# Statistics of x first, x1's normed rows made late on VectorE, values' products ahead of the maxima, in a fused GNN and attention kernel

## The chip, the cores and the metric

One NeuronCore of a Trainium2 chip runs the program. The metric is the device time in microseconds of one execution. TensorE is PE here (PEld its weight loads), VectorE is DVE, ScalarE is ACT, GpSimd is POOL, and SP issues all the DMAs.

## The reference

x has 1250 rows (nodes) of 512. What is computed, cut to what matters:

```
xn = layernorm(x)
x1 = x + relu(xn @ W_self.T + mean_of_neighbours(xn) @ W_neigh.T + b)      # 41250 edges
       + linear_attention(xn) @ W_out.T + b_out                            # softmax of k over rows
z  = layernorm(x1)                                   # input of the last block
route = softmax(gelu(mean_rows(z) @ r1.T + b) @ r2.T + b)   # picks one spatial, one temporal expert
s = spatial_expert(ln(z)); t = temporal_expert(ln(z))       # 8 heads of 64, temporal one causal
z = z + cross_attention(s, t)
out = x1 + z + mlp(ln(z))                            # 512 -> 2048 -> 512
```

## The kernel before

Rows lie in ten tiles of 125 (`NT`), features in four blocks of 128. Precise products are made of three: every operand is split into a rounded part (hi) and the rest (lo), and hi*hi, hi*lo and lo*hi are added in PSUM. POOL splits the weights: it casts `w_raw` to `w_hi` (L893) and subtracts (L895); SP loads them three slots ahead. Semaphores order everything; each engine's program is a fixed list.

**Start.** SP issues the edges, x in three transfers (blocks of 4, 4 and 2 tiles, `TB`), `vecs`, six one-row transfers into `raw_rows`, then the weights. VectorE makes the edge keys, waits for the six rows (L1527), makes `row_mix`, `row_gnn` and `ones_r` of them (L1528 to L1534), and only then the statistics of x (`bn_stats`, L1538), the aggregates, with a square root on ScalarE in between (L1084), and ten normed tiles (L1448, `normed`). `to_feature` on PE (L1926) turns them into features through two PSUM banks (6 and 7), ScalarE copies the hi part (L1092), VectorE subtracts for the lo part (L1458). Then the first key products run (L1975).

**Edges.** Forty windows: VectorE makes one-hot rows (L1558, L1559), PE counts with them (L2076), and side products of the linear attention and the GNN are placed between. x1 is in `kept`; VectorE takes its statistics. The last tile's neighbour sum (`neighbours`, L2042) has `set_turn` (L1941) placed between its parts: these turn `set_rows`, x1 normed twice, into features, copied by `set_in` on ScalarE and `set_lo_in` on VectorE.

**Router.** POOL makes x1's normed rows z into `tok_b` (L982, nine tiles; VectorE makes the tenth). PE takes their mean with a column of 1/1250 (L2107), VectorE copies it out (L1638), two small products, a gelu and a softmax follow; SP reads the two expert numbers into registers and loads the experts' biases and weights. `tok_b` is also stored to DRAM (`d_xn`, 2000 KB at L776 and 500 KB at L811), since z is added again near the end. x1 itself is stored to `d_x1`.

**Passes.** Twelve passes of two heads each (0 to 3 spatial, 4 to 7 temporal, 8 to 11 cross) with up to 50 steps (S scores, P products with the values), planned by due times. Each pass needs keys (K, three pieces), queries (Q, five tiles), values (V, three pieces), maxima (M, ten for a query tile), their row turned (R, L2227) and the values turned (T). Inside a run of passes these are spread over the steps of the pass before. Passes 0 and 8 have no pass before them, so an order written out by hand opens them (`OPENING`); PE's waits there are for ScalarE's copies of the keys (L1221) and VectorE's reductions of the maxima (L1718, L1727). A head pair's output of a query tile is scaled by `unit_out` on VectorE (L1735, L1737).

**End.** When all queries are made, SP loads `tok_z` from `d_xn` and `bias_out`; POOL adds the bias to each tile (L1034). The last output goes through `oc_hi` (ScalarE), `oc_lo` (VectorE, L1818), the projection (L2328), the sum with `tok_z` (L1828), a layer norm and the MLP.

Of the kernel before, what the change touches and what calls it, by code (L numbers as in the profile page):

```python
# [6 lines left out]
F32 = mybir.dt.float32  # L7
# [11 lines left out]
TOK = 125  # L19
# [138 lines left out]
def value_turns(n):  # L158
# [4 lines left out]
OPENING = {n: [("K", n, 0), ("K", n, 1), ("K", n, 2), ("Q", n, 0)] + maxima(n, 0)[0:2] + [("V", n, 0)] + maxima(n, 0)[2:4] + [("V", n, 1)]  # L163
           + maxima(n, 0)[4:6] + [("V", n, 2)] + maxima(n, 0)[6:8] + [("Q", n, 1)] + maxima(n, 0)[8:] + [("R", n, 0)] + value_turns(n)
# [151 lines left out]
def load_order():  # L316
# [12 lines left out]
    events += [(AT["F", x], 0, ("fold", x)) for x in range(FB)] + [(AT["Q", 3, 4], 0, ("xt",)), (28, 0, ("store",)), (-1, NO["v", 0] + 0.5, ("rows",))]  # L329
# [59 lines left out]
def build(nc, A, out):  # L389

    ctx = ExitStack()
    with ctx:
# [111 lines left out]
        tok_b = sb("tok_b", [TOK, NT, D], F32, tok_b_at)  # L504
        set_rows = sb("set_rows", [TOK, NT, D], F32)
# [5 lines left out]
        mean_col = sb("mean_col", [TOK, 1], F32)  # L511
# [113 lines left out]
        s_tok = sem("s_tok")  # L625
# [111 lines left out]
        def _(sp):  # L737
# [5 lines left out]
            sp.dma_start(vecs[:, :], A["vecs"]).then_inc(s_ld_vec, 16)  # L743
# [14 lines left out]
            for k in range(16):  # L758
                weights(k, block_of("w_gps", k))
# [15 lines left out]
            sp.wait_ge(s_tok, 8)  # L775
            sp.dma_start(d_xn[:, 0:8, :], tok_b[:, 0:8, :]).then_inc(s_st_xn, 16)  # L776
# [21 lines left out]
            for what, *at in LOADS:  # L798
# [9 lines left out]
                if what == "rows":  # L808
                    sp.wait_ge(s_tok, FIRST_ROWS)
                    sp.wait_ge(s_ln_done, 2 * NT - 1)  # L810
                    sp.dma_start(d_xn[:, 8:NT, :], tok_b[:, 8:NT, :]).then_inc(s_st_xn, 16)  # L811
# [15 lines left out]
            sp.wait_ge(s_st_xn, 32)  # L827
            sp.dma_start(tok_z[:, :, :], d_xn).then_inc(s_xn_back, 16)
# [36 lines left out]
        def _(pool):  # L865
# [79 lines left out]
            pool.memset(mean_col[:, :], 1.0 / NODES).then_inc(s_const, 1)  # L945
# [52 lines left out]
            pool.wait_ge(s_st_xn, 32)  # L998
# [77 lines left out]
        def _(act):  # L1076
# [9 lines left out]
            def features_in():  # L1086

                m = 0
                for t0, nt in TB:
                    for f in range(FB):  # L1090
                        act.wait_ge(s_tr, m + 1)
                        act.activation(xa_hi[:, f, t0 * TOK:(t0 + nt) * TOK], ps[:, 6 + m % 2, 0:nt * TOK], ACT.Copy).then_inc(s_tr_act, 1)  # L1092
                        m += 1

            def set_in(m):
# [6 lines left out]
                if f == FB - 1:  # L1102
                    act.wait_ge(s_st_first, 16)
                    act.wait_ge(s_tok, 2)
                act.activation(z_feat[:, f, span], src, ACT.Copy).then_inc(s_tr_act, 1)

            ln_root(0)
# [213 lines left out]
            act.wait_ge(s_st_xn, 32)  # L1321
# [84 lines left out]
        def _(dve):  # L1406
# [44 lines left out]
            def features_lo():  # L1451

                m = 0
                for t0, nt in TB:
                    for f in range(FB):
                        span = slice(t0 * TOK, (t0 + nt) * TOK)
                        dve.wait_ge(s_tr_act, m + 1)
                        dve.tensor_tensor(xa_lo[:, f, span], ps[:, 6 + m % 2, 0:nt * TOK], f32(xa_hi[:, f, span]), ALU.subtract)\  # L1458
# [1016 lines left out]
```

## Time and profile before

| what | value |
|---|---|
| runs | 1999.69, 1993.12, 1999.56 us; median 1999.56 |
| profiled execution | 1993.96 us; span 1992.2 us |
| mean granted TensorE clock | 0.977 |
| PE busy | 1824.9 us, 92% |
| DVE, ACT, POOL busy | 1181.7, 723.5, 356.4 us |
| DMA | 60.56 MB, 30 GB/s on the mean |

The span runs from the first to the last instruction of the profiled execution. Times in the rows are counted from its start. In a timeline row the first two numbers are start and duration; "x8" means that eight instructions in a row are merged; the bracket tells how long the engine was idle before and what ended that. In the chain, each piece is what the end of the program hung on at that time.

### The profile page before, as it was taken

To read this page: it belongs to the slowest core of one execution; us is meant where nothing else is said; L and a number is where in the kernel's file an instruction comes from. 1 tells how busy PE (TensorE), PEld (TensorE's weight loads), DVE (VectorE), ACT (ScalarE), POOL (GpSimd) and SP (SyncE) were. 2 spreads that over 40 slices of the span, in tenths; PEclk is the share of its full clock that TensorE was granted. 3 is DMA by queue.
4 is the path that set the end of the run, shared out by engine and by line. 5 is a ranking of instruction groups with operands and counts; after the bars stand their busy time and mean duration, and the time that the engine had idled before them with its cause. 6 is when DMAs were issued, how large, how long until landed. Compare 5 with 4: busy or idle time off the path is not lost.

```text
span 1992.2 us, 30956 instructions
## 1 busy us (share of the span) xinstructions
PE 1824.9 (92%) x10475; PEld 1625.9 (82%) x10475; DVE 1181.7 (59%) x2333; ACT 723.5 (36%) x1345; POOL 356.4 (18%) x345
## 2 busy tenths in 40 slices
PE   1899989976899999999999899989999999999998
PEld 0678657864799989989888898879999999788996
DVE  6577558775556546563746657556656566576332
ACT  0223211013565435445544454245545444221110
POOL 3210001015121102020100002200000003455440
PEclk9999989987999999999999999999999999999999
DMA  3101000012020100011000000100000001212111
GB/s 107 32 6 43 11 6 30 8 47 94 12 115 27 32 22 11 1 69 58 11 12 11 12 1 1 38 11 12 6 8 9 6 1 44 72 36 64 43 32 52
DMA packets 25043, 60.56 MB, mean 30 GB/s; under 512 B 2548, under 2 KB 4816, under 8 KB 24149
## 3 DMA queue, kind: packets, MB, share of 16 engines
q1 hardware_dynamic: 24910, 58.74, 8.9%
q8 instruction: 90, 1.47, 0.3%
q14 instruction: 43, 0.34, 0.1%
HBM read 44.87 MB, written 13.86 MB: 29 GB/s over the span
## 4 chain that ended last, share of the span: by engine, by line
PE 78%; DVE 11%; issue 3%; POOL 2%; ACT 2%; DVEq 1%; DMA 1%; SPq 1%; POOLq 0%; ACTq 0%
PE ps L2273 19%; PE ps L2158 13%; PE ps L2328 7%; PE ps L1962 5%; PE ps L2255 5%; PE ps L2259 5%; PE ps L2216 5%; PE ps L2357 4%; DVE max_part L1718 4%; PE ps L2076 3%; PE ps L2042 3%; DVE share L1735 2%; PE ps L1975 2%; PE ps L2284 1%; POOL tok_b L982 1%
## 5 line engine op out<-in xcount | busy, mean ns | idle before, releaser
L2273 PE MATMUL ps<-p_raw,v_ones 125*128 125x250 f32 x2080 | 527.3, 375 | 10.5 <-DVE feat L1737 8.4
L1718 DVE TENSOR_REDUCE max_part<-ps 125x2 f32<-125x500 f32 x520 | 330.4, 674 | 246.0 <-PE ps L2216 233.7
L1294 ACT ACTIVATE p_raw<-ps 125x500 f32<-125x500 f32 x520 | 304.3, 586 | 350.9 <-PE ps L2259 346.2
L2273 PEld LDWEIGHTS ps<-p_raw,v_ones 125*128 125x128 f32 x2080 | 360.9, 190 | 37.0 <-issue 9.8
L1735 DVE RECIPROCAL share<-ps 64x250 f32<-64x250 f32 x120 | 206.3, 1719 | 79.5 <-PE ps L2273 76.6
L2255 PE MATMUL ps<-q_both_a,k_both_a 128*125 128x250 f32 x520 | 183.5, 373 | 1.8 <-ACT q_row_b L1268 1.8
L2255 PE MATMUL ps<-q_both_b,k_both_b 128*125 128x250 f32 x520 | 182.0, 371 | 0.0
L893 POOL CAST w_hi<-w_raw 128x512 fp32r<-128x512 f32 x44 | 28.1, 638 | 814.0 <-issue 359.7
L2158 PE MATMUL ps<-xa_hi,w_hi 128*128 128x418 f32 (+1 forms) x448 | 151.4, 338 | 19.8 <-POOL w_lo L895 14.0
L1559 DVE TENSOR_SCALAR onehot<-iota_h,win_key,key_t 125x320 f16 x453 | 169.1, 373 | 0.8 <-issue 0.6
L1558 DVE TENSOR_SCALAR onehot<-iota_h,low_t 125x125 f16 x453 | 127.6, 282 | 58.5 <-PE ps L2076 30.0
L2216 PE MATMUL ps<-k_both_a,q_both_a 128*125 128x250 f32 x520 | 139.7, 287 | 19.4 <-ACT k_both_b L1221 9.1
L2158 PE MATMUL ps<-xa_lo,w_hi 128*128 128x418 f32 (+1 forms) x448 | 148.7, 332 | 0.0
L2158 PE MATMUL ps<-xa_hi,w_lo 128*128 128x418 f32 (+1 forms) x448 | 148.7, 332 | 0.0
L2216 PE MATMUL ps<-k_both_b,q_both_b 128*125 128x250 f32 x520 | 139.8, 286 | 0.0
L2259 PE MATMUL ps<-q_row_a,k_rest_a 65*125 65x250 f32 x520 | 139.1, 288 | 0.0
L2259 PE MATMUL ps<-q_row_b,k_rest_b 128*125 128x250 f32 x520 | 137.0, 285 | 0.0
L2216 PEld LDWEIGHTS ps<-k_both_a,q_both_a 128*125 128x125 f32 x520 | 97.7, 188 | 22.6 <-issue 19.2
L2158 PEld LDWEIGHTS ps<-xa_hi,w_hi 128*128 128x128 f32 x448 | 86.7, 193 | 23.0 <-issue 14.3
L2076 PE MATMUL ps<-onehot 125*125 x453 | 86.4, 310 | 20.7 <-DVE onehot L1559 20.1
L2255 PEld LDWEIGHTS ps<-q_both_a,k_both_a 128*125 128x125 f32 x520 | 98.1, 189 | 8.2 <-issue 2.2
L2259 PEld LDWEIGHTS ps<-q_row_a,k_rest_a 65*125 65x125 f32 x520 | 98.6, 190 | 5.9
(375 smaller groups left out, 3423.4 us busy)
## 6 DMA issues: line engine op xcount, KB each, us to landing
w_raw<-in_w_mlp SPq DMA_DIRECT2D x32, 256.0 KB, 2.6
w_raw<-in_w_gps SPq DMA_DIRECT2D x16, 256.0 KB, 2.7
w_raw<-in_w_tp SPq DMA_DIRECT2D x16, 256.0 KB, 2.6
w_raw<-in_w_sp SPq DMA_DIRECT2D x12, 256.0 KB, 2.7
w_raw<-in_w_cr SPq DMA_DIRECT2D x12, 256.0 KB, 2.6
d_xt<-xb_hi SPq DMA_DIRECT2D x1, 2508.0 KB, 7.5
d_xt<-xb_lo SPq DMA_DIRECT2D x1, 2508.0 KB, 14.9
xa_hi<-d_xt SPq DMA_DIRECT2D x1, 2508.0 KB, 9.5
```

The costliest lines, as they stand in the source:

```text
L1294: act.activation(p_raw[:, g % PR, :], ps[0:TOK, g % 2, 0:4 * TOK], ACT.Exp, scale=SCALE).then_inc(s_exp, 1)
L1558: dve.tensor_scalar(row[:, 0:ET], iota_h[0:ET, 0:ET], low, None, ALU.is_equal)
L1559: ins = dve.tensor_scalar(row[:, ET:ET + DH], iota_h[0:ET, :], win_key[0:ET, bass.ds(w, 1)], key, ALU.add, ALU.is_equal)
L1718: dve.tensor_reduce(part[:, y, :, j], ps[0:TOK, bank, 0:4 * TOK].rearrange("p (h k) -> p h k", h=2), AX.X, ALU.max)\
L1735: dve.reciprocal(share[own, :], ps[other, 2 + u % 2, 0:2 * TOK]).then_inc(s_share, 1)
L2076: ins = pe.matmul(ps[0:ET, bank, 0:DH], row[:, 0:ET], row[:, ET:ET + DH], start=(first and c == 0), stop=(last and c == CH - 1), skip_grou ...
L2158: ins = pe.matmul(ps[:, bank, 0:width], w[:, ROLE_SLOT[role], 128 * c:128 * c + 128], x[:, c, first:first + width], start=(c == 0 and y == ...
L2216: ins = pe.matmul(to, q_both[h][:, ring(n, i), tile], k_both[h][:, n % 2, keys], start=True, stop=not masked)
L2255: pe.matmul(to, k_both[h][:, n % 2, tile], q_both[h][:, ring(n, i), :], start=True, stop=False)
L2259: ins = pe.matmul(to, k_rest[h][rest, n % 2, tile], q_row[h][rest, ring(n, i), :], start=False, stop=True)
L2273: ins = pe.matmul(ps[:, bank, 0:2 * TOK], v_ones[:, n % 2, kt, h:h + 2, :], p_raw[:, g % PR, cols], start=(b == 0 and x == 0), stop=last)
L2328: ins = pe.matmul(ps[0:TOK, bank, :], x[:, c, t * TOK:(t + 1) * TOK], w[:, c, :], start=(c == 0 and n == 0), stop=(c == FB - 1 and n == 2))
```

## The change

Four things.

1. Start: the statistics of x come right behind the edge arithmetic on VectorE, the bias rows' operations behind the lo parts of x; the first three weights are issued ahead of `vecs` and the row transfers; a square root of nothing ahead of ScalarE's real one; `to_feature` goes through four banks (6, 7, 0, 1).
2. Router: `tok_b`, its nine POOL tiles, VectorE's tenth and both stores are gone. `pooled_row` takes the mean with x1 itself: the column is 1/sigma of the tile, and a second product of one column gives the sum of mean/sigma, which VectorE subtracts. Rows 0 and 1 stand between the parts of the last neighbour sum, and the turns begin two parts later; rows 2 to 9 come behind turns 6 and 7. The waits for `d_xn`'s stores are gone.
3. Openings of passes 0 and 8: V0 and V1 come before the first maxima, V2 behind three, Q1 behind six.
4. End: `tok_z` is loaded from `d_x1`, VectorE makes z of it in place (ten tiles, `XN_AT`, steps 515 to 519 of 520), and POOL's add of a tile waits for that tile.

```diff
-OPENING = {n: [("K", n, 0), ("K", n, 1), ("K", n, 2), ("Q", n, 0)] + maxima(n, 0)[0:2] + [("V", n, 0)] + maxima(n, 0)[2:4] + [("V", n, 1)]
-           + maxima(n, 0)[4:6] + [("V", n, 2)] + maxima(n, 0)[6:8] + [("Q", n, 1)] + maxima(n, 0)[8:] + [("R", n, 0)] + value_turns(n)
+OPENING = {n: [("K", n, 0), ("K", n, 1), ("K", n, 2), ("Q", n, 0), ("V", n, 0), ("V", n, 1)] + maxima(n, 0)[0:3] + [("V", n, 2)] + maxima(n, 0)[3:6]
+           + [("Q", n, 1)] + maxima(n, 0)[6:] + [("R", n, 0)] + value_turns(n)
...
+        X_BANK = (6, 7, 0, 1)
+        XN_AT = {FIRST[11, 4] + 5 + x: (2 * x, 2 * x + 1) for x in range(NT // 2)}
...
-            sp.dma_start(vecs[:, :], A["vecs"]).then_inc(s_ld_vec, 16)
...
+            for k in range(3):
+                weights(k, block_of("w_gps", k))
+            sp.dma_start(vecs[:, :], A["vecs"]).then_inc(s_ld_vec, 16)
             sp.wait_ge(s_zero, 1)
...
-            sp.wait_ge(s_tok, 8)
-            sp.dma_start(d_xn[:, 0:8, :], tok_b[:, 0:8, :]).then_inc(s_st_xn, 16)
             sp.wait_ge(s_x1, NT)
...
-            sp.wait_ge(s_st_xn, 32)
-            sp.dma_start(tok_z[:, :, :], d_xn).then_inc(s_xn_back, 16)
+            sp.wait_ge(s_st, 64)
+            sp.wait_ge(s_st_first, 16)
+            sp.dma_start(tok_z[:, :, :], d_x1).then_inc(s_xn_back, 16)
...
-            pool.wait_ge(s_ln, 16)
-            for t in range(FIRST_ROWS):
-                pool.tensor_scalar(tok_b[:, t, :], kept[:, t, :], ln_mv[:, t, 0:1], ln_r[:, 1, 0, t:t + 1], ALU.subtract, ALU.mult)\
-                    .then_inc(s_tok, 1)
...
-            pool.wait_ge(s_xn_back, 16)
             pool.wait_ge(s_ld_bias, 16)
             for t in range(NT):
+                pool.wait_ge(s_xn, t + 1)
                 pool.tensor_tensor(tok_z[:, t, :], tok_z[:, t, :], bias_out[:, :], ALU.add).then_inc(s_resid, 1)
...
+            act.activation(small[:, 0:1], small[:, 5:6], ACT.Sqrt)
             ln_root(0)
             features_in()
...
-            dve.wait_ge(s_ld_row, 96)
-            dve.tensor_copy(row_mix[:, :], raw_rows[:, 0, :]).then_inc(s_row, 1)
-            dve.tensor_copy(row_gnn[:, :], raw_rows[:, 1, :]).then_inc(s_row, 1)
-            dve.memset(raw_ones[:, :], 1.0).then_inc(s_row, 1)
-            dve.wait_ge(s_row, 3)
-            for p, row, x in ((32, row_mix, 0), (96, row_mix, 0), (32, row_gnn, 1)):
-                dve.tensor_tensor(row[p:p + 1, :], raw_rows[p:p + 1, x, :], f32(row[p:p + 1, :]), ALU.subtract).then_inc(s_row, 1)
-            dve.tensor_copy(ones_r[:, :], raw_ones[:, :]).then_inc(s_row, 1)
             for t in range(NT):
                 if t in (0, 4, 8):
...
             features_lo()
+            dve.wait_ge(s_ld_row, 96)
+            dve.tensor_copy(row_mix[:, :], raw_rows[:, 0, :]).then_inc(s_row, 1)
+            dve.tensor_copy(row_gnn[:, :], raw_rows[:, 1, :]).then_inc(s_row, 1)
+            dve.memset(raw_ones[:, :], 1.0).then_inc(s_row, 1)
+            dve.wait_ge(s_row, 3)
+            for p, row, x in ((32, row_mix, 0), (96, row_mix, 0), (32, row_gnn, 1)):
+                dve.tensor_tensor(row[p:p + 1, :], raw_rows[p:p + 1, x, :], f32(row[p:p + 1, :]), ALU.subtract).then_inc(s_row, 1)
+            dve.tensor_copy(ones_r[:, :], raw_ones[:, :]).then_inc(s_row, 1)
...
-            normed(tok_b, kept, 9, 0)
             normed(set_rows, kept, 8, 1)
...
-            dve.tensor_copy(pool_row[:, :], ps[0:1, 5, :]).then_inc(s_route, 1)
+            dve.tensor_copy(route[:, 60:61], ps[0:1, 0, 0:1]).then_inc(s_shift, 1)
+            dve.wait_ge(s_shift, 1)
+            dve.tensor_scalar(pool_row[:, :], ps[0:1, 5, :], route[:, 60:61], 1.0 / NODES, ALU.subtract, ALU.mult).then_inc(s_route, 1)
...
+                    if g in XN_AT:
+                        dve.wait_ge(s_xn_back, 16)
+                        for t in XN_AT[g]:
+                            dve.tensor_scalar(tok_z[:, t, :], tok_z[:, t, :], ln_mv[:, t, 0:1], ln_r[:, 1, 0, t:t + 1], ALU.subtract, ALU.mult)\
+                                .then_inc(s_xn, 1)
...
-                        if m >= 2:
-                            pe.wait_ge(s_tr_dve, m - 1)
+                        if m >= 4:
+                            pe.wait_ge(s_tr_dve, m - 3)
...
+            def pooled_row(t):
+
+                if t == 0:
+                    pe.wait_ge(s_ln, 16)
+                    pe.wait_ge(s_sum_in, 8)
+                if t == FIRST_ROWS:
+                    pe.wait_ge(s_ln, 24)
+                pe.matmul(ps[0:1, 5, :], ln_r[:, 1, 0, t:t + 1], kept[:, t, :], start=(t == 0), stop=(t == NT - 1))
+                ins = pe.matmul(ps[0:1, 0, 0:1], ln_r[:, 1, 0, t:t + 1], ln_mv[:, t, 0:1], start=(t == 0), stop=(t == NT - 1))
...
+                    if turns and x == 3:
+                        pooled_row(0)
+                        pooled_row(1)
...
-                neighbours(NT - 1, part, (2, 3, 4, 5, 6, 7, 8, 9))
+                neighbours(NT - 1, part, (4, 5, 6, 7, 8, 9))
+            set_turn(6)
+            set_turn(7)
...
+            for t in range(2, NT):
+                pooled_row(t)
             set_turn(8)
```

## Rows read from the trace of the kernel before

**Rows 1.** The page, busy time by engine (share of the span, instructions)

```profile
PE 1824.9 (92%) x10475; PEld 1625.9 (82%) x10475; DVE 1181.7 (59%) x2333; ACT 723.5 (36%) x1345; POOL 356.4 (18%) x345
```

**Rows 2.** The chain that ended last, 0 to 120 us: start, us, what

```profile
17.91 9.43 DMA raw_rows<-in_rows_gps
...
33.44 5.95 DVE ln_stats L1538 x10
...
40.59 1.28 ACT L1084
...
43.30 4.65 DVE tok_a L1448 x10
...
60.24 9.56 PE ps L1975 x36
```

**Rows 3.** Timeline from 0 to 75 us, and the answer on L1458

```profile
15.30 0.15 DVE L1526 COPY small<-small 128x1 f32<-128x1 f32 x1
...
27.65 0.61 POOL L893 CAST w_hi<-w_raw 128x512 fp32r<-128x512 f32 x1 [22.99 <-DMA w_raw<-in_w_gps]
...
L1458 DVE TENSOR_TENSOR xa_lo<-ps,xa_hi x12: 417/674/680, 47.9 to 59.7; 128x500 fp32r<-128x500 f32 x8, 128x250 fp32r<-128x250 f32 x4
```

**Rows 4.** The chain that ended last, 436 to 520 us

```profile
442.97 20.60 POOL tok_b L982 x9
...
463.61 1.89 PE ps L2107 x4
...
479.82 5.14 DMA w_raw<-in_w_sp
...
487.19 10.84 PE ps L2158 x48
...
507.08 0.47 PE ps L2216 x4
...
507.55 2.29 PE ps L2158 x12
...
513.06 1.40 PE ps L2158 x12
...
516.46 1.28 DVE max_part L1718 x2
...
518.15 0.39 PE ps L2227 x2
```

**Rows 5.** TensorE's waits: us in total, times, longest

```profile
PE ps L2216 <- ACT k_both_b L1221: 9.1, 2, 4.5
```

**Rows 6.** Timeline from 1692 to 1735 us, and the answer on L1818

```profile
1706.33 13.04 POOL L1034 TENSOR_TENSOR tok_z<-tok_z,bias_out 125x512 f32<-125x512 f32 x10 [17.72 <-DMA bias_out<-in_bias_out]
...
1708.24 0.41 DVE L1737 TENSOR_TENSOR feat<-ps,share 64x250 f32<-64x250 f32 x1
...
1712.66 1.71 DVE L1735 RECIPROCAL share<-ps 64x250 f32<-64x250 f32 x1 [4.01 <-PE ps L2273]
...
L1818 DVE TENSOR_TENSOR oc_lo<-feat,oc_hi x3: 1199/1664/1671, 1715.4 to 1718.2; 128x418 fp32r<-128x418 f32 x3
```

**Rows 7.** One microsecond of windows (DMA share and GB/s are last)

```profile
26.00:27.00 1.00, 0.00 (x0) 0.00 (x0) 0.00 (x0) 0.00 (x0) 0.00 (x0) 1.00 0.33 127
```

**Rows 8.** Timeline at 72 us, and L1558 from 69 to 82 us

```profile
72.48 1.39 POOL L895 TENSOR_TENSOR w_lo<-w_raw,w_hi 128x512 fp32r<-128x512 f32 x1
...
L1558 DVE TENSOR_SCALAR onehot<-iota_h,low_t x8: 243/611/1286, 71.8 to 80.6; 125x125 f16 x8
```

**Rows 9.** The answer on L1448: min, median, max in ns

```profile
L1448 DVE TENSOR_SCALAR set_rows<-kept,ln_mv,ln_r x10: 533/924/984, 442.9 to 462.4; 125x512 f32<-125x512 f32 x10
```

**Rows 10.** Timeline from 428 to 505 us, TensorE

```profile
455.29 7.12 PE L2107 MATMUL ps<-tok_b,mean_col 125*1 125x512 f32 x16
```

**Rows 11.** DMA issues from 455 to 495 us

```profile
d_xn<-tok_b SPq DMA_DIRECT2D x1, 2000.0 KB
```

**Rows 12.** The page, DMA issues: KB each, us to landing

```profile
w_raw<-in_w_gps SPq DMA_DIRECT2D x16, 256.0 KB, 2.7
```

More of the change, by code:

```diff
@@ L328, in load_order @@
         events.append((g, k, ("w", *name)))
-    events += [(AT["F", x], 0, ("fold", x)) for x in range(FB)] + [(AT["Q", 3, 4], 0, ("xt",)), (28, 0, ("store",)), (-1, NO["v", 0] + 0.5, ("rows",))]
+    events += [(AT["F", x], 0, ("fold", x)) for x in range(FB)] + [(AT["Q", 3, 4], 0, ("xt",)), (28, 0, ("store",))]
     return [event[2] for event in sorted(events)]
@@ L501, in build @@
         assert place["end"] <= near_at + 4 * NT * (D - 128)
-        tok_b = sb("tok_b", [TOK, NT, D], F32, tok_b_at)
-        set_rows = sb("set_rows", [TOK, NT, D], F32)
+        set_rows = sb("set_rows", [TOK, NT, D], F32, tok_b_at + 20480)
         norm_tmp = sb("norm_tmp", [128, 2, 4 * TOK], F32, feat_at)
@@ L624, in build @@
         s_xb_tmp = sem("s_xb_tmp")
-        s_tok = sem("s_tok")
+        s_pool_rows = sem("s_pool_rows")
+        s_xn = sem("s_xn")
+        s_shift = sem("s_shift")
         s_st_first = sem("s_st_first")
@@ L757, in _ @@
                 sp.dma_start(raw_rows[p:p + 1, x, :], A["rows_gps"][y:y + 1, :]).then_inc(s_ld_row, 16)
-            for k in range(16):
+            for k in range(3, 16):
                 weights(k, block_of("w_gps", k))
@@ L807, in _ @@
                     weights(NO[at[0], at[1]], block_for(*at))
[L808 to L811, printed above, removed]
                 if what == "store":
@@ L997, in _ @@
                 split_next(role, 0)
-            pool.wait_ge(s_st_xn, 32)
             pool.wait_ge(s_tmp, 12)
@@ L1091, in features_in @@
                         act.wait_ge(s_tr, m + 1)
-                        act.activation(xa_hi[:, f, t0 * TOK:(t0 + nt) * TOK], ps[:, 6 + m % 2, 0:nt * TOK], ACT.Copy).then_inc(s_tr_act, 1)
+                        act.activation(xa_hi[:, f, t0 * TOK:(t0 + nt) * TOK], ps[:, X_BANK[m % 4], 0:nt * TOK], ACT.Copy)\
+                            .then_inc(s_tr_act, 1)
                         m += 1
@@ L1457, in features_lo @@
                         dve.wait_ge(s_tr_act, m + 1)
-                        dve.tensor_tensor(xa_lo[:, f, span], ps[:, 6 + m % 2, 0:nt * TOK], f32(xa_hi[:, f, span]), ALU.subtract)\
+                        dve.tensor_tensor(xa_lo[:, f, span], ps[:, X_BANK[m % 4], 0:nt * TOK], f32(xa_hi[:, f, span]), ALU.subtract)\
                             .then_inc(s_tr_dve, 1)
@@ L1655, in _ @@
             dve.wait_ge(s_route, 7)
-            dve.wait_ge(s_const, 11)
+            dve.wait_ge(s_const, 10)
             for h in range(2):
@@ L1797, in _ @@
                 query_lo(n, 0)
-                for task in largest[:8]:
+                for task in largest[:6]:
                     maximum(*task[1:])
                 query_lo(n, 1)
-                for task in largest[8:]:
+                for task in largest[6:]:
                     maximum(*task[1:])
@@ L1933, in set_turn @@
                 (t0, nt), f = TB[m // FB], m % FB
-                pe.wait_ge(s_ln_done, NT + (4, 8, 11)[m // FB])
+                pe.wait_ge(s_ln_done, NT + (4, 8, 10)[m // FB])
                 if m < 4:
@@ L2028, in side @@
                 ins.then_inc(s_side, 1)
+            def pooled_row(t):
[6 more added lines that the diff above has]
+                ins = pe.matmul(ps[0:1, 0, 0:1], ln_r[:, 1, 0, t:t + 1], ln_mv[:, t, 0:1], start=(t == 0), stop=(t == NT - 1))
+                if t == 1:
+                    ins.then_inc(s_pool_rows, 1)
+                if t == NT - 1:
+                    ins.then_inc(s_pool_mm, 1)
             def neighbours(t, part, turns=()):
@@ L2097, in _ @@
             for part in range(3):
-                neighbours(NT - 1, part, (2, 3, 4, 5, 6, 7, 8, 9))
-            pe.wait_ge(s_const, 11)
-            pe.wait_ge(s_sum_in, 8)
-            for t in range(NT):
-                if t < FIRST_ROWS:
-                    pe.wait_ge(s_tok, t + 1)
-                else:
-                    pe.wait_ge(s_ln_done, 2 * NT - 1)
-                ins = pe.matmul(ps[0:1, 5, :], mean_col[:, :], tok_b[:, t, :], start=(t == 0), stop=(t == NT - 1))
-            ins.then_inc(s_pool_mm, 1)
+                neighbours(NT - 1, part, (4, 5, 6, 7, 8, 9))
[3 more added lines that the diff above has]
+                pooled_row(t)
             set_turn(8)
```

7 lines of the change are left out of this document (2 added, 5 removed).

## The prediction

> **What bounds the kernel now.** I read the page first: TensorE (PE) is busy 92% of the span [rows 1], so what can be won lies where PE stands still. The view of waits and the chain of waits give four such places; the rest is not touched by the diff. One: from 0 to 60.24 PE does almost nothing. The chain there runs through the bias rows' transfer (17.91 to 27.34), then L1528 to L1534 on VectorE, then the statistics of x (33.44 to 39.4), a table load of 1.28, the ten normed tiles, and the loop of transposes, ScalarE copies and VectorE differences [rows 2]. The edge arithmetic on VectorE is over at 15.30, POOL splits weights from 27.65 [rows 3]. Two: the router, whose chain goes through POOL's nine normed rows, the ones-column matmuls, L1638, and ends in a weight transfer of 5.14 and PE's restart at 487.19 [rows 4]. Three: the opening of passes 0 and 8, where PE waits 4.5 for ScalarE's copy of the keys, both times [rows 5]. Four: the end of pass 11, where VectorE's last share (L1735 at 1712.66) sets when the projection starts [rows 6].
>
> **Start.** VectorE now turns to bn_stats at 15.30 and waits for x instead. x is three transfers of 125 partitions; while they run the DMA share stands at 0.33 and 127 GB/s, to the last full microsecond [rows 7]. 2.56 MB at 127 GB/s is 20.2 us, from about 2.5: 22.7 at the earliest; at the latest 27.3, as the bias rows, issued behind x, landed at 27.34 [rows 2]. I take 25.5. Eight tiles are done by then, the last two take 2 x 0.6 = 1.3. From the end of bn_stats to the first normed tile it was 43.30 - 39.4 = 3.9; the table load of 1.28 now happens ahead of it: 2.6 [rows 2]. So the first normed tile starts at 29.4 instead of 43.30. There it ran with POOL idle, 4.65 for ten; now POOL splits weights beside it. What that costs no row shows exactly. Below: nothing. Above: L1558, 0.25 alone, took 1.29 while a POOL difference of 1.39 ran [rows 8], and three VectorE operations per POOL block (0.6 + 1.3) come to 1.1 each, 11 for ten. Nearest in form is the same instruction beside POOL's tensor_scalar: 0.92 instead of 0.54 [rows 9]. I take 9. From the last normed tile to the first key product it was 60.24 - 47.95 = 12.3. With four banks in place of two PE no longer waits for each difference: the first four groups are turned while VectorE still norms, and VectorE's 8 x 0.67 + 4 x 0.42 = 7.1 [rows 3] plus the last group's hand-over sets it: 8.5. Sum: 29.4 + 9 + 8.5 = 47 against 60.24: **-13.5**. Bounds: 22.7 + 3.9 + 4.65 + 8.5 = 40, -20; 27.3 + 3.9 + 11 + 9 = 51, -9. The bias rows' casts, now behind the differences, cost nothing: 5.5 long, under 9.56 of key products [rows 2], where VectorE waits for the keys anyway; without that cover they would cost 5.5. Weights 0 to 2, issued ahead of vecs, land right behind x, so only the first is nearly late; the values need the fifth block, 9.6 us of products later. SP's six row transfers and vecs move behind them; the first reader of vecs is ScalarE after the keys. The edge stage then shifts as a whole, since all its waits are among the engines.
>
> The Trainium skill ("DMA: Bandwidth & Descriptors", section "Why a DMA increments its semaphore by 16 and not by 1") says that a transfer uses the largest number of engines up to 16 that divides its partitions, 5 for 125. The trace agrees with 0.33 of 16; by 5/16 of the page's peak of 436 GB/s I estimate 136 GB/s and x at 21, a gain larger by 4.
>
> **Router.** POOL's rows fall away; PE forms sum of r*x directly from kept, with a one-column product for the shift beside each. It was 0.89 a row (7.12 for eight) [rows 10]; the added product is two passes over one column, which I estimate at 0.1 each, so 1.1. Two rows now stand ahead of the turns in the last tile's sum: ScalarE's first copy comes 3 us later, and VectorE's sum_in(9) stands behind four differences that wait for it, 2 us later. On PE the rows began at 455.29; the last tile's sum, with two rows more and two turns fewer ahead of it, ends about 1 later, and three turns instead of one follow it (a turn is four transposes, taken as 0.5): eight rows of 1.1 run from 457.3 to 466.1, where the ten ended at 463.61 + 1.89 = 465.5 before [rows 4, 10]. L1638 becomes a copy of one element and a tensor_scalar: +0.25. So pool_row is ready 1 us later than now (0 to 2). Against that stand the DMAs: the store of d_xn, 2000 KB issued once POOL's eighth row is there (442.97 + 8/9 of 20.60 = 461.3), and half a MB behind it, at 127 GB/s keep the part of the DMA engines that such a store uses busy until about 481 [rows 4, 7, 11], and the first key weights land 5.14 after their issue, 2.7 where the queue is free [rows 4, 12]. Nothing is stored there now: -2.4 for the landing, and I take -3 with the three issues in front of it, which shared the queue. Sum **-2** (-3.5 to +1). POOL's memsets and VectorE's k_rest shift with POOL's splits.
>
> **Openings.** PE ends Q0 at 487.19 + 10.84 = 498.0. New: V0 and V1, 2.29 each, cover the copies until 502.6; three maxima at 0.47; V2 to 506.4; three maxima to 507.8; Q1 (1.4) to 509.2; four maxima to 511.1. Q1's copy and difference take 2.0 (514.46 to 516.46), four reductions 0.64 each, the column 0.2: 514.0. The max row is turned at 514.1 instead of 518.15 [rows 4]. That is -4.05, and twice: **-8.1**. No bank is late: V0 to V2 take the banks of K0 to K2, whose differences ended a product earlier, and the later maxima find theirs reduced 1 us or more before. Bounds -9 and -6 (a maximum's reduction in the way of Q1's difference).
>
> **End.** tok_z is now loaded from d_x1, the same bytes at the same place in the queue, and VectorE makes ten normed tiles. All five pairs stand between unit 118's share (ends at 1708.24 + 0.41 = 1708.65) and the last unit's, which starts at 1712.66 [rows 6]. Without contention: 4.65, to 1713.3, 0.6 late. But each tile releases POOL's add of that tile, 1.3 long [rows 6]. Beside those very adds L1818 took 1.66 (1.2 to 1.67); two tiles free and eight at 1.66 give 14.2, to 1722.9: 10.2 late. At 0.85 a tile, from the tensor_scalar beside POOL [rows 9], it is 4.5 late. The row nearest in place and in POOL's operation is the slow one, nearest in VectorE's the other: I take **+8** (+0.6 to +11, the last with PE coming back at half clock for longer). What is late next: oc_hi, oc_lo, the first projection. POOL's own splits for the MLP, behind the adds, are read only after the ten projections.
>
> The Trainium skill ("SBUF — State Buffer", section "SBUF: two separate sides") has VectorE and GpSimd share one port pair under a lock that is held for a whole instruction, for VectorE's two-port modes or two SBUF inputs. L1558's 1.29 agrees, the 0.92 of L1448 beside a POOL operation of over 2 us does not fully. By the rule alone the time would be C's of the rivals below.
>
> **Sum.** -13.5 - 2 - 8.1 + 8 = **-15.6**. The profiled run took 1993.96, and the runs fall at two levels, 1993 and 1999.6, the median at the upper. I set the sum against the middle of the two, 1996.6: **1981** (1978.4 against the profiled run's own time, 1984 against the median).
>
> **Rivals.** A: as summed, 0.50, 1972 to 1989. B: the normed tiles hardly feel POOL: start -18, end +0.6, the rest as above, -27.5, **1969**; for it speaks that ten tiles at 0.54 are the rule elsewhere; against it L1558 and L1448 beside POOL [rows 8, 9]. Chance 0.25. C: VectorE and POOL take turns one for one in both places, as L1818 did beside POOL's adds: eleven for the tiles at the start (-11.5), 10.2 late at the end: -11.4, **1985**, and 1988 if x lands only at 27.3. For it speaks that L1818 ran in the very place; against it L1448's 0.92. Chance 0.21. D, slower: VectorE stands at its new wait for the load of tok_z, with the last unit's share queued behind it. Each microsecond past 1708.65 counts in full; it cancels the 23.6 gained before, and 10 more, only if the load lands after 1732, with the tiles 14.2 behind it: **2007** or more. Against it: the bias, issued behind that load, had landed at 1706.33 [rows 6]. 0.04. That the change does nothing at the start is as good as excluded, since the bias rows stood on the chain.
>
> About 0.5% (10 us) is what a measurement tells here from no change. Faster by more than that: nearly all of A, B, and half of C, which reaches across the bound of 1989.6: 0.80; within it 0.16; slower 0.04. The range takes in A to C, and their bounds on either side: 1964 to 1996.
>
> **What would show it.** First key product at 40 to 51, I say 47; bn_stats ending at 27; the tiles on tok_a at about 0.9. pool_row within 2 us of its place relative to the end of the edge stage, key weights landing 2.7 after issue. From the end of Q0 to the max row's turn 16 instead of 20, in passes 0 and 8. In pass 11 ten tensor_scalars between the two last shares, at 0.8 to 1.7 each. Wrong it would be if the tiles were stretched by a wait for the load, or if the edge stage took up the start's gain.

## The result, and the profile after

The changed kernel took 1967.04 us (median of 4 runs, 1965.32 to 1968.53) where the kernel before took 1999.62 in the same session: a ratio of 0.9851, 95% interval [0.9838, 0.9865]. The profiled execution took 1968.53 with a span of 1966.7, 25.4 less than before's span of 1992.2. So it is faster by more than 0.5%, as given a chance of 0.80, and inside the range, but 14 us under the forecast of 1981. Of these 14, 9.8 are the sum's (25.4 measured on the profiled executions against 15.6), 2.6 come from setting the sum against 1996.6, and 1.5 from the profiled execution being slower than the median. The medians lie further apart than the two profiled executions, since the runs of before fall at 1993 and at 1999.6 to 2000.4; what follows explains the 25.4 us between the profiled ones.

The same work, located in both traces, gives the gain by stage. Each row is the time gained between one point and the next, so the column adds up to 25.4.

| from the point above to | before | after | gained | forecast |
|---|---|---|---|---|
| first key product | 60.24 | 50.30 | 9.94 | 13.5 |
| end of the edge stage (its last one-column product) | 439.80 | 428.05 | 1.81 | 0 |
| copy that yields the pooled row | 465.52 | 451.73 | 2.04 | -1 |
| first product of pass 0 | 487.19 | 468.50 | 4.90 | 3 |
| turn of the max row, pass 0 | 518.15 | 493.33 | 6.13 | 4.05 |
| last share of pass 7 | 1258.75 | 1234.52 | -0.59 | 0 |
| turn of the max row, pass 8 | 1320.53 | 1291.10 | 5.20 | 4.05 |
| last share of pass 10 | 1635.14 | 1606.83 | -1.12 | 0 |
| last share of pass 11 | 1712.66 | 1684.91 | -0.56 | -8 with the next |
| end of the span | 1992.17 | 1966.74 | -2.32 | |

The page of the changed kernel, busy time by engine, against [rows 1]:

```profile
PE 1820.8 (93%) x10495; PEld 1624.1 (83%) x10495; DVE 1184.8 (60%) x2343; ACT 723.6 (37%) x1346; POOL 337.7 (17%) x335
```

PE is busy for 4 us less and the span is 25 shorter: what was won is idle time, as the forecast had it.

**Start.** The chain of the changed kernel, 0 to 60 us, against [rows 2]:

```profile
3.40 24.82 DMA tok_a<-in_x
28.24 1.30 DVE ln_stats L1523 x2
...
31.66 1.26 DVE ln_r L1430
...
33.71 1.13 DVE ln_r L1436
...
34.87 8.30 DVE tok_a L1441 x10
...
43.90 3.58 PE ps L1925 x16
...
50.30 7.11 PE ps L1974 x36
```

The bias rows are off the chain and x is on it. x landed at 28.24, later than my latest bound of 27.3; in the eight other kernels that load x the same way behind this start it was 27.2 to 28.5. Two small operations of the scale took 1.26 and 1.13 (0.19 in e8 below, where POOL stands). The ten tiles took 8.30, near the 9 forecast. The timeline of the same kernel shows POOL's side of it:

```profile
31.62 1.26 POOL L894 TENSOR_TENSOR set_lo<-w_raw,set_hi 128x512 fp32r<-128x512 f32 x1
...
33.51 1.28 POOL L894 TENSOR_TENSOR set_lo<-w_raw,set_hi 128x512 fp32r<-128x512 f32 x1
...
35.43 1.32 POOL L894 TENSOR_TENSOR set_lo<-w_raw,set_hi 128x512 fp32r<-128x512 f32 x1
```

Each long operation of VectorE ends just behind a difference of POOL's. What came back was not forecast: the first 14 key products. The windows of before, then of the changed kernel (busy time and count of PE first):

```profile
60.24:65.00 4.76, 4.76 (x14) 4.54 (x15) 0.00 (x0) 0.21 (x1) 0.00 (x0) 1.00 0.00 0
```

```profile
50.30:53.00 2.70, 2.69 (x14) 2.67 (x15) 2.60 (x6) 0.14 (x1) 0.00 (x0) 1.00 0.00 0
```

The same 14 products took 4.76 us before and 2.70 now. They follow each other at 0.35 us before and at 0.19 now, and these are the distances of the products of the same width at the opening of pass 0 under a granted clock of 0.50 and of 1.00: the lower and the upper level of PE's clock. The 1.00 in the first row measures nothing: the first record of the clock in before's trace is a rise to full at 65.6 us, and a window without a record is printed as 1.00. In the changed kernel that first rise is at 48.7, ahead of the keys. Before, the transposes came in groups of eight with gaps between; now 24 ran from 43.90 nearly without one. The gain does not follow from that alone. e1 has the same start and runs 20 transposes without a gap, its clock rises at 41.8, and it falls again at 48.6, where the keys begin:

```profile
48.46:52.30 3.84, 3.84 (x12) 3.67 (x13) 2.98 (x8) 0.00 (x0) 0.00 (x0) 0.56 0.00 0
```

The 36 products of the first keys took 9.56 in before, 7.1 in changed, e3 and e7 to e11, and 8.65 in e1, e4, e5, e6 and e12.

**Router and opening.** The chain of the changed kernel, 427 to 496 us, against [rows 4]:

```profile
451.73 0.75 DVE pool_row L1632
...
463.56 2.72 DMA w_raw<-in_w_sp
...
468.50 14.69 PE ps L2169 x72
483.19 0.88 PE ps L2227 x6
484.07 2.28 PE ps L2169 x12
...
487.06 1.41 PE ps L2169 x12
...
490.47 2.45 DVE max_part L1712 x4
...
493.33 0.60 PE ps L2238 x2
```

POOL's 20.60 us of rows are gone, the first key block lands after 2.72 instead of 5.14, and from the key products to Q1 PE stands nowhere: the wait of [rows 5] is in no answer of the changed kernel any more.

**End.** Timeline of the changed kernel, 1680 to 1700 us, against [rows 6]:

```profile
1680.24 4.64 DVE L1809 TENSOR_SCALAR tok_z<-tok_z,ln_mv,ln_r 125x512 f32<-125x512 f32 x10
1684.91 1.72 DVE L1729 RECIPROCAL share<-ps 64x250 f32<-64x250 f32 x1
...
1680.91 17.28 POOL L1026 TENSOR_TENSOR tok_z<-tok_z,bias_out 125x512 f32<-125x512 f32 x10 [20.62 <-DVE tok_z L1809]
```

VectorE's ten tiles were not stretched at all; POOL's ten adds took 17.28 instead of 13.04. The answer on POOL's line shows where (min, median, max in ns):

```profile
L1026 POOL TENSOR_TENSOR tok_z<-tok_z,bias_out x10: 1262/1284/5086, 1680.9 to 1696.9; 125x512 f32<-125x512 f32 x10
```

One of them, the first, took 5.09: it ran out 1.1 us behind VectorE's last tile.

### The profile page after: what moved, and what is told of

The parts are those of the page before. It is cut to its first block, busy times and chain, and to the rows that moved or that the text cites. A ratio compares the mean times of both kernels' runs of the same rounds, so it can differ in the third digit from the quotient of the medians.

```text
span 1966.7 us, 30993 instructions
## 1 busy us (share of the span) xinstructions
PE 1820.8 (93%) x10495; PEld 1624.1 (83%) x10495; DVE 1184.8 (60%) x2343; ACT 723.6 (37%) x1346; POOL 337.7 (17%) x335
## 4 chain that ended last, share of the span: by engine, by line
PE 79%; DVE 12%; issue 3%; DMA 2%; ACT 1%; DVEq 1%; POOL 1%; SPq 0%; POOLq 0%; ACTq 0%
PE ps L2284 19%; PE ps L2169 13%; PE ps L2339 7%; PE ps L1961 6%; PE ps L2266 5%; PE ps L2270 5%; PE ps L2227 5%; PE ps L2368 4%; DVE max_part L1712 4%; PE ps L2055 3%; PE ps L2092 3%; DVE share L1729 2%; PE ps L1974 1%; PE ps L2295 1%; DMA tok_a<-in_x 1%
## 5 line engine op out<-in xcount | busy, mean ns | idle before, releaser
L2270 PEld LDWEIGHTS ps<-q_row_b,k_rest_b 128*125 128x125 f32 x520 | 97.7, 188 | 6.0
```

The source lines that it names most:

```text
L2270: ins = pe.matmul(to, k_rest[h][rest, n % 2, tile], q_row[h][rest, ring(n, i), :], start=False, stop=True)
```

## Experiments

Before and changed stand for the two kernels. The edits are given in outline. The changed kernel's times are those of the result above; e1 to e12 ran in other sessions, in which before took 1994.2 to 1995.0 (median), so small differences are read from the stages of the traces as well.

**e1: the start alone**, in the kernel before.

```diff
-  dve: bias rows; bn_stats; scale; tiles; features_lo
+  dve: bn_stats; scale; tiles; features_lo; bias rows
-  transposes in banks 6, 7
+  transposes in banks 6, 7, 0, 1
-  sp: x, vecs, rows, weights 0..15
+  sp: x, weights 0..2, vecs, rows, weights 3..15
+  act: Sqrt ahead of ln_root(0)
```

> The kernel before with only the start changed (statistics of x ahead of the bias rows, weights 0 to 2 ahead of vecs, four banks for the transposes, the early square-root table). Theory 1, from the trace of after: the start is worth what the end of the edge stage showed, 11.75 us earlier, and nothing later gives it back or adds to it: 11 to 12.5 us less than before, first key product at 50 to 50.6 us instead of 60.24, and keys over at about 57.5. Theory 2, the prediction's step: 13.5 us. Theory 3, the stages are not independent (the edge stage owes part of its 11.75 to another edit of the change): clearly under 10 us.

Median 1984.92 against 1994.22, ratio 0.9951 [0.9933, 0.9968]. First key product at 48.46, end of the edge stage at 428.13 (-11.67, as in changed), first product of pass 0 at 475.34 (-11.85). The 11.67 is made up otherwise than in changed: the first key product is 1.84 earlier than there, and the stretch from it to the end of the edge stage is 379.67, as in before (379.56), and not 377.75, since the keys ran at the lower clock. At the end of the span only 6.65 of it are left. The rest is lost on the way: 0.3 in pass 0's opening, 0.9 in pass 0, 1.4 in pass 7, 1.1 in pass 8's opening, 0.9 behind it, 0.6 behind the last share. Theory 1 holds for the stage, not for the end; the time, 9.3 less than before, is in theory 3's range, but its reason is excluded by the end of the edge stage. More on that under e2.

**e2: the openings alone**, in the kernel before (the line OPENING and VectorE's 6 for 8).

> The kernel before with only the order of passes 0 and 8's openings changed. Theory 1, from the trace of after: from the keys' first product to the turn of the max row each opening is 5 to 6 us shorter, so 10 to 11 us less in all, of which 4 each is the order itself and the rest PE running at full clock where it stood still and fell to half before; the first projection of the last pass is not touched. Theory 2, the prediction's step: 8.1 us, and the excess seen in after comes from the router's side (weights that landed earlier). Theory 3: part is given back later in the passes, since a later unit waits for the values or for POOL: 4 to 7 us.

Median 1987.48, ratio 0.9963 [0.9949, 0.9977]. Max row's turn of pass 0 at 513.03, 5.1 earlier; pass 8's opening gains 5.2 more. That is the 10 to 11 of theory 1, and 6.3 is left in the span; 6.3 is in theory 3's range, but its reason, a unit that waits, is not what the windows show. Windows of passes 5 and 6 in before, then in e2:

```profile
1043.27:1124.90 81.63, 75.50 (x494) 71.07 (x493) 49.94 (x72) 40.16 (x78) 5.66 (x6) 1.00 0.04 11
1124.90:1206.41 81.51, 75.39 (x494) 70.96 (x493) 49.93 (x71) 40.14 (x78) 1.89 (x2) 1.00 0.01 4
```

```profile
1037.86:1121.02 83.16, 77.04 (x494) 72.54 (x493) 49.94 (x72) 40.16 (x78) 5.66 (x6) 0.98 0.04 10
1121.02:1203.92 82.90, 76.81 (x494) 72.13 (x493) 49.92 (x72) 40.14 (x78) 1.89 (x2) 0.98 0.02 4
```

The same 494 products, with VectorE and ScalarE as busy as before, took 1.5 and 1.4 longer at a granted clock of 0.98 instead of 1.00. No edit touches these passes. A stage's gain is real in the stage and can be partly lost where the granted clock falls in a pass that was left alone. Pass 7 took 52.3 at 1.00 in eight kernels, before and changed among them, and 53.7 to 53.9 at 0.97 in e1, e3, e6, e7, e8 and e12. In changed no such loss fell into passes 1 to 7. Another one is in every kernel but before: from the turn of the max row to the end of pass 0 before took 111.73 and the others 112.4 to 112.9, in pass 8 it took 110.06 and the others 110.7 to 111.2. e1, which keeps the old openings, loses 0.9 in each, so this is not the price of the new order. Why the clock falls there is open.

**e3, e5, e6: the router.** e3 puts a store of 2000 KB back, e5 a second one of 500 KB, e6 (without stores) POOL's nine rows.

```diff
 e3   sp.dma_start(d_x1[:, 8:NT, :], kept[:, 8:NT, :])
+     sp.wait_ge(s_tr_dve, TR2 + 5)
+     sp.dma_start(d_xn[:, 2:NT, :], kept[:, 2:NT, :])
 e5  (e3, and behind key block 2)
+     sp.dma_start(d_xn[:, 0:2, :], kept[:, 8:NT, :])
 e6
+     pool.wait_ge(s_ln, 16); nine tensor_scalar tok_b<-kept
```

> The changed kernel with a store of 2000 KB of x1's rows (tiles 2 to 9, read by nobody) put back on SP's queue right behind the last store of x1, at about the place relative to the router at which the normed rows were stored before, with ScalarE's and POOL's waits for it. Theory 1: the store is what made SP's register loads (2.9 us), the vectors' issue (1.43) and the landing of the first key weights (5.14) slow in the kernel before; then the run is 3.5 to 5 us slower than the changed kernel, with PE's restart at 472 to 473.5 us instead of 468.5. Theory 2, the prediction's step: about 3 us. Theory 3: register loads and issue are slow for another reason (POOL's rows of that time) and the landing is hidden: under 1 us.

> The kernel of e3_store_again with the second store as well, 500 KB (tiles 8 and 9) issued behind the third key block's load, where the kernel before had it. In e3 the stretch from SP's register loads to PE's first key product was 9.70 us (in the changed kernel 7.58, in the kernel before 12.47). Theory 1: what is left of the difference is this second store, which runs beside the first key block: 12 to 12.6 us. Theory 2: it is issued too late to matter for the first block and the rest has another cause (the queue still busy with other bytes): 9.5 to 10.2.

> The changed kernel in which POOL makes nine normed rows again where it made them before (nobody reads them; the first two are of tiles 2 and 3 once more). Measured from the end of the edge stage (428.05 in the changed kernel, 439.80 before) to the copy that yields the pooled row: 23.68 in the changed kernel, 25.72 before; the prediction had 1 us more than before. Theory 1: VectorE's part beside POOL's rows (set_rows at 924 ns instead of 542, the small operations of the scale) is what was lost before, so with the rows back the stretch is 25 to 26 and set_rows run at 0.85 to 1.0 us. Theory 2: the stretch is PE's, whose rows come off kept directly: 23.5 to 24, even with slower set_rows. Either way POOL's 20.6 us of rows end before the key blocks land.

| stretch | before | changed | e3 | e5 | e6 |
|---|---|---|---|---|---|
| end of edge stage to pooled row | 25.72 | 23.68 | 23.63 | 24.36 | 24.75 |
| pooled row to SP's register loads | 9.20 | 9.19 | 9.18 | 9.18 | 10.01 |
| register loads to first product | 12.47 | 7.58 | 9.70 | 9.71 | 7.53 |

e3's median was 1971.92, 4.9 above changed's, and so in theory 1's range, but its span is only 2.3 longer: 2.1 in the last row of the table, where theory 1 had 3.5 to 5, and 1.4 in pass 7 at a clock of 0.97, less 1.1 at the start. From before to changed the last row fell by 4.9 us, and the store accounts for 2.1 of them: the chain of e3 has tp_vecs's issue at 1.28 (0.37 in changed, 1.43 before) and

```profile
464.00 3.24 DMA w_raw<-in_w_sp
```

It is 2.72 in changed and 5.14 before. So the store gives back 1.6 of the 2.5 us from SP's register loads to the issue of the first key block, and only 0.5 of the 2.4 us of the landing, which was the prediction's step. The second store changes nothing, since it is issued behind the first block; theory 2 of e5. The other 2.8 us of that stretch no run gave back. In e3 the 2000 KB had the 500 KB of d_x1 ahead of them and in before behind, and in the windows from the store on they moved at 124 to 133 GB/s in e3 and 109 to 129 in before; whether that is the whole of it stays open. e5 and e6 were one run each (1972.78 and 1973.03). e6 gives back 1.1 ahead of the pooled row and 0.8 behind it; its answer on the rows of VectorE is theory 1's, its stretch lies between the two theories: set_rows took 5.82 for eight beside POOL (3.74 in changed). The first row of the table has a spread of its own: with the router unchanged it is 23.6 to 23.7 in six kernels at a granted clock of 0.94, and 24.4 to 24.5 in e5, e7, e8 and e12 at 0.91. e6 ran at 0.94, so its 1.1 is counted against 23.68.

**e7, e8, e9: x and POOL at the start.**

```diff
 e7
-  sp.dma_start(tok_a[:, t0:t0 + nt, :], x_dram[:, t0:t0 + nt, :])
+  for p0, p1 in ((0, 112), (112, TOK)):
+      sp.dma_start(tok_a[p0:p1, t0:t0 + nt, :], x_dram[p0:p1, t0:t0 + nt, :])
 e8
   split_next("mk", 0)
+  pool.wait_ge(s_ln_done, NT)
   split_rows("mv", set_hi, set_lo)
 e9  both
```

> The changed kernel with each of x's three transfers cut into two, partitions 0 to 111 and 112 to 124. In the changed kernel they ran at a DMA share of 0.33 and 125 GB/s, and the last block was waited for until 28.24. Theory 1: the share depends on the number of partitions, and with 112 it goes to 0.9 or more: x has landed before VectorE turns to the statistics at 15.4, which then end at 21.6 instead of 29.5; the first normed tile starts at 25.5 to 27.5, the first key product at 42 to 44, and the run is 6 to 8 us faster than the changed kernel. The Trainium skill (DMA: Bandwidth & Descriptors, section Why a DMA increments its semaphore by 16 and not by 1) has a transfer use the largest divisor of its partitions up to 16: 16 and 13 engines. Theory 2: the rate is that of x's rows in DRAM, whatever the partitions: no change, within 1 us, or 1 us slower by three more issues on SP.

> The changed kernel in which POOL splits the first key block as before and then waits for the ten normed tiles. In the changed kernel POOL's splits of 29.0 to 41.1 lay beside the scale's small operations (1.25, 1.12, 0.62 and 0.52 for some that take 0.18 alone) and the ten tiles (8.30 for ten; 4.6 where POOL gave way or stood). Theory 1: both were POOL's: the first normed tile starts at 32.3 to 33, ten take 4.6, and the first key product comes at 45 to 46.5 instead of 50.3; the value products then wait for their blocks for 0 to 3 us, and the run is 2 to 5 us faster than the changed kernel. Theory 2: the splits only move on and now stretch VectorE's differences out of PSUM (8 x 0.67 and 4 x 0.42 in the changed kernel, with POOL idle), so the first key product comes at 48 to 51 and the run is within 2 us of the changed kernel.

> The changed kernel with the edits of e7_x_112 and e8_pool_held together. In e7 POOL's splits lay from 17.57 to 29.1, beside the scale's small operations (21.42 to 27.22, where e8 without POOL beside them needed 2.95) and the first tiles (5.82 for ten, 4.65 in e8). Theory 1, both add: first normed tile at 24.4, first key product at 35.5 to 36 instead of 39.7, the five other blocks split from 29 to 39, before the values' products at 43; the run is 3 to 5 us faster than e7, so 1953 to 1955 us. Theory 2: with the keys that early the values' products wait for the fourth block, or PE's first products fall at half clock for longer: under 2 us faster than e7.

e7: 1958.03, ratio 0.981 [0.9794, 0.9826]. Windows of e7 (the last two columns are the DMA share and GB/s):

```profile
3.00:9.00 6.00, 0.09 (x1) 0.12 (x1) 5.08 (x13) 0.00 (x0) 1.66 (x5) 1.00 1.03 248
9.00:15.00 6.00, 2.33 (x10) 1.44 (x10) 4.97 (x18) 0.00 (x0) 0.00 (x0) 1.00 1.07 223
```

The share went from 0.33 [rows 7] to over 1 and the rate doubled; VectorE's statistics ran in one piece from 15.37 to 21.4, and the first key product came at 39.69, 2.3 ahead of what theory 1 gave. So the form of the load was the limit, not x's rows. No run cut x in another way (100 and 25, say); against the rival that it is the number of transfers speaks that changed's three, all issued by 10.1 us, stood at 0.33. By the Trainium skill (DMA: Bandwidth & Descriptors, section Why a DMA increments its semaphore by 16 and not by 1) a transfer uses the largest divisor of its partitions up to 16; the trace agrees for 125 (0.33) and for 112 (1.03 to 1.07).

e8: 1959.97, ratio 0.9822 [0.9805, 0.9838]. Its chain at the start, POOL waiting:

```profile
30.70 0.19 DVE ln_r L1431
...
31.33 0.19 DVE ln_r L1437
...
31.55 1.92 DVE tok_a L1442 x4
...
33.61 5.25 PE ps L1926 x24
...
42.84 7.10 PE ps L1975 x36
```

The small operations fall to 0.19 and the ten tiles from 8.30 to 4.65, and the differences out of PSUM, now beside POOL's splits, still take 0.64 each (3.21 for five). That is 7.5 us at the first key product: 2.4 by the scale, 3.65 by the tiles, 0.5 behind them, and 1.0 because x landed earlier in this execution. e9: 1954.20, ratio 0.9797 [0.9781, 0.9813], its interval clear of changed's: faster than both kernels. First key product at 34.78, 15.5 ahead of changed. In each of the three it is theory 1's mechanism that came; e9's gain over e7, 3.8 us, is in its range, those of e7 (9.0 against 6 to 8) and e8 (7.1 against 2 to 5) are above theirs.

**e4, e12, e10, e11: who gives way at the end.** e4 computes another residual (tok_z times the bias instead of the normed tile); e12 adds three sums of POOL's that nobody reads.

```diff
 e4
-  dve.tensor_scalar(tok_z[:, t, :], tok_z[:, t, :], mean, r, subtract, mult)
+  dve.tensor_tensor(tok_z[:, t, :], tok_z[:, t, :], bias_out[:, :], mult)
 e12
+  pool.wait_ge(s_share, 119)
+  three tensor_tensor tok_x[:, t, :] <- bias_out + bias_out
   for t in range(NT): pool.wait_ge(s_xn, t + 1) ...
 e10
-  XN_AT = {FIRST[11, 4] + 5 + x: ...}
+  XN_AT = {FIRST[11, 4] + x: ...}    and tok_z loaded as 112 + 13 partitions
 e11  e9 and e10
```

> The changed kernel in which the ten tiles made late in pass 11 are a product of two SBUF operands (tok_z times bias_out) instead of tok_z with two columns; so x1's residual is another one, and the wait for the bias row's load stands ahead of them too. In the changed kernel ten tiles took 4.64 us in one piece while POOL's adds of the same time took 1.73 each. Theory 1: an operation with one full SBUF operand holds out against POOL's adds, one with two takes turns with them: ten tiles take 12 to 17 us (1.2 to 1.7 each), the projection starts 8 to 12 us later, and the run is 8 to 12 us slower than the changed kernel: the +8 that the prediction put on the tiles would have been right for this form. Theory 2: it is not the form, the two operations simply have the same length as alone (0.69 each, as the other additions of two operands of this size): 7 us for ten, 2.3 us slower. Theory 3: POOL gives way in either form: under 3 us slower, with POOL's adds at 1.7 or more.

> The changed kernel in which POOL makes three additions of its own (of the bias with itself, read by nobody) from the moment at which unit 118's reciprocal is done, some 0.4 us ahead of the ten normed tiles, so that POOL is at work when VectorE comes to them. In the changed kernel the tiles were first: ten took 4.64 us without a gap, and POOL's first addition, started 0.14 us behind the second tile, took 5.09 us and ended 1.12 after the last tile; at the start of the kernel POOL was first, and VectorE's tiles took turns with it (0.76, 1.48, 0.83, 1.48). Theory 1: whoever is at work when the other comes decides. Then the tiles take turns with POOL's additions here too: 1.2 to 1.7 each, 9 to 14 us in all, with POOL's additions at 1.3 to 1.7 each: the prediction's +8 for the other order of arrival. Theory 2: at this place a run of VectorE's operations wins whenever it has begun: the first tile waits up to 1.3 us, the other nine take 0.46 to 0.53 each and POOL's next addition 5 us. Theory 3: it depends on the operation of POOL, and against its additions VectorE is never held up: all ten at 0.53.

> The changed kernel with the load of tok_z in two pieces (partitions 0 to 111, 112 to 124) and the five pairs of normed tiles one unit earlier, in VectorE's idle stretch ahead of unit 118's share (4.4 us at 1673.8). In the changed kernel the load ran 2500 KB at 115 to 143 GB/s and the key blocks behind it landed at 1679, so the tiles could not have stood there. Theory 1: the load lands by 1670, the tiles run uninterrupted before 1678.4, the last share starts with its product at about 1684.3 instead of 1684.91, and the run is 0.5 to 1.5 us faster than the changed kernel (the first projection at half clock for no longer). Theory 2: the tiles wait for the load, or POOL's adds, now beside more of VectorE's shares and reductions, stretch these: 0 to 4 us slower.

> The changed kernel with the edits of e7, e8 and e10 together. If the gains add: e9's time less 0.5 to 1.5 us, so 1952 to 1954 us, faster than both kernels. If e10's half costs: e9's time or up to 4 us more.

e4: 1969.72. Ten in 6.09, POOL's first add 6.40 long, the last share 1.5 later than in changed: theories 2 and 3, the form isn't it. e12, timeline of VectorE and POOL:

```profile
1681.27 13.27 DVE L1812 TENSOR_SCALAR tok_z<-tok_z,ln_mv,ln_r 125x512 f32<-125x512 f32 x10
...
1681.04 3.40 POOL L1026 TENSOR_TENSOR tok_x<-bias_out 125x512 f32<-125x512 f32 x3 [19.72 <-DVE share L1732]
1684.40 13.71 POOL L1029 TENSOR_TENSOR tok_z<-tok_z,bias_out 125x512 f32<-125x512 f32 x10
```

One run, 1977.32. With POOL at work 0.2 us ahead, the same ten tiles take 13.27, one for one with POOL's sums (1.48 against 1.44 each), and the stretch from pass 10's last share to pass 11's is 8.6 us longer than in changed; the span is 8.8 longer. Theory 1. e10, with the tiles one unit earlier, 1972.05, ratio 0.9891 [0.9872, 0.991]:

```profile
1673.67 12.31 DVE L1810 TENSOR_SCALAR tok_z<-tok_z,ln_mv,ln_r 125x512 f32<-125x512 f32 x10
...
1674.36 13.96 POOL L1027 TENSOR_TENSOR tok_z<-tok_z,bias_out 125x512 f32<-125x512 f32 x10 [14.19 <-DVE tok_z L1810]
```

Its load had landed in time, VectorE was first by 0.69 us, as in changed by 0.67, and yet they took turns from the third tile on. So the order of arrival alone does not decide. In all eight kernels with the tiles at changed's place and POOL idle when they began VectorE held, in both with them one unit earlier it didn't; what makes the difference is open. e10 costs 3.1 us in the span, and e11, at 1957.31 (ratio 0.9812 [0.9798, 0.9826]), is 3.1 slower than e9 for the same reason. Theory 2 in both, by contention and not by the load.

## Why the prediction was right, and where it was off

The direction and the four places were right. Of the sum's terms one was too large, two too small, and one was priced for a case that did not come. The router, the openings and the end came out better than their terms by 13.3 together, the start was 1.7 smaller, and the passes, for which the sum had nothing, gave back another 1.7. So the errors lean one way, and the time lies near the lower end of the range.

- **Start, -13.5; measured -9.94 at the first key product and -11.75 at the end of the edge stage.** Three parts of it missed. x at 25.5: it was 28.24. Weights 0 to 2, which I let land "right behind x", are issued beside it; that they delay it is not shown, since no run is without them, and e7 shows that the load's form was the larger matter. "From the end of bn_stats to the first normed tile 2.6": it was 5.35 (29.52 to 34.87), since I let POOL stretch the tiles and not the scale ahead of them; e8, with POOL standing, needed 2.98. The ten tiles at 9 (8.30) and the tail at 8.5 (7.1) were near. What came back is the 2.06 us of the first 14 products, which I had not in the sum; with the same start it came in changed, e3 and e10 and only in part in e1, e4, e5, e6 and e12, so it is partly luck.
- **Router, -2; measured -6.94.** "Ready 1 us later" was 2.04 earlier: the rows ran at 0.9 and not at 1.1, and I had taken VectorE's part as it was beside POOL's rows; e6 gives 1.1 of it back. The landing, -3, was -4.90 with SP's register loads and tp_vecs's issue, which I hadn't named; e3 shows 2.1 of it as the store's, 2.8 stay open.
- **Openings, -8.1; measured -6.13 and -5.20.** The order of the steps was as forecast: from Q0's end at 478.6 to the turn 14.7 against 16 (20.15 before). The mis-sized term is "three maxima at 0.47": the 0.47 of [rows 4] is that of x4 products, which are two maxima, so I had each at twice its price. Three took 0.88 and 0.70, and Q1 was over 1.3 sooner. With 0.235 for each of the six, the sum's -4.05 becomes -5.5, and the traces give -5.4 from Q0's end. The other 0.7 of pass 0's -6.13 lies ahead of it, in the key products (10.10 against 10.81): 9 of them ran at the lower clock and 14 before. e2 alone gives 5.1 and 5.2, so that much is the openings' own.
- **End, +8; measured +0.56 to the last share, +2.32 behind it.** The step that failed is "beside those very adds L1818 took 1.66; two tiles free and eight at 1.66". The bound without contention held to a tenth (0.56 late against 0.6). e12 shows that the mechanism and its price exist (13.27 for ten against the 14.2 that I had worked out): rivals A and C are right for the case in which POOL is first. It was the case that I chose wrongly, not the size; what decides between the cases is open, as e10 shows. The 2.32 behind it is mostly PE's clock: windows of the first down block in before, then in changed:

```profile
1817.07:1846.52 29.45, 29.45 (x121) 23.57 (x122) 7.49 (x10) 0.00 (x0) 6.70 (x6) 0.95 0.11 36
```

```profile
1790.12:1821.05 30.93, 30.93 (x121) 24.59 (x122) 7.50 (x10) 0.00 (x0) 6.69 (x6) 0.90 0.11 34
```

The same 121 products take 1.5 longer at 0.90. Another 0.66 is in the first projections (21.95 against 21.29 for 84). The 1.5 is not the tiles' doing: e9, with the same code and the tiles at the same place, has before's clock there,

```profile
1774.02:1803.44 29.42, 29.42 (x121) 23.54 (x122) 7.49 (x10) 0.00 (x0) 6.70 (x6) 0.95 0.12 36
```

and from the last share to the end it takes 280.11 against 281.83 in changed. e1 and e2, which make no tiles there, take 280.15 and 280.28, before 279.51.

B was the nearest rival in time (1969) but by the wrong reason at the start, where the tiles did feel POOL; D didn't come.

By the rule of the Trainium skill (SBUF — State Buffer, section SBUF: two separate sides) the one that starts first has the shared ports for the whole instruction, if VectorE's is in a two-port mode or has two SBUF inputs; that the tiles' instruction ran in such a mode no trace shows. e12, e8 and the start of the changed kernel agree (1.48 a tile beside POOL, 0.53 alone); that a run of ten tiles kept POOL's add for over 4 us, and that it did not in e10, the rule doesn't give.

## What to carry to other kernels

A transfer whose partition count has no large divisor may be worth cutting in two: here 125 into 112 and 13 was worth 9.5 us of the span, over a third of what the whole change gave. When a chain on VectorE is freed, ask what POOL does beside it, the small operations included, and hold POOL back by one wait if its work is not due. Price contention with both orders of arrival, and keep both for the range; read each stage's gain from its own two ends, since the granted clock can take back some us elsewhere.

## What the runs showed that I had not expected

- A run of VectorE operations without a gap kept one POOL operation for its whole length (5.09 us for an add of 1.28; 6.40 in e4), while POOL at work first made the same operations take turns (1.48 instead of 0.53), and in e10 and e11 they took turns though VectorE was first.
- Two operations on 20 columns took 1.26 and 1.13 instead of 0.19 beside POOL's splits: small ones pay as much as large ones.
- 14 products at 4.76 and at 2.70 us, with 1.00 printed as the granted clock of both: ahead of the first record of the clock (65.6 us in before) the figure says nothing.
- Passes that no edit touches were 1.4 to 1.5 us longer in some kernels, at a granted clock of 0.97 or 0.98.
